# The causal mask of decayed attention: added by VectorE to the scores in place, instead of by mask products on TensorE

## The chip, the cores and the metric

The kernel runs on one core of a Trainium2 chip. The metric is the device time of one execution in microseconds (us). One launch computes a whole small network; the change touches its last stage alone, about 210 us of some 1860 us.

Engines are named as the profile names them: PE is TensorE's matrix products, PEld its weight loads (they overlap PE), DVE is VectorE, ACT is ScalarE, POOL is GpSimd, SP is the queue that issues DMAs.

## The reference, cut to what matters

The last stage computes two layers, an attention with a decay and a ternary projection, each followed by a residual sum and a layer norm. B is 8 sequences of N = 256 tokens (the layer takes them as the network has them), 128 channels, 16 heads of 8 channels:

```python
q = pi * _rotate(q, cos, sin) + (1.0 - pi) * q
k = pi * _rotate(k, cos, sin) + (1.0 - pi) * k
decay = -e * d_mat[None, :, :] / xi[:, None, None]
causal = jnp.where(pos[:, None] >= pos[None, :], 0.0, -jnp.inf)
bias = decay + causal[None, :, :]
scores = jnp.einsum('bhqd,bhkd->bhqk', q, k) * dh ** (-0.5) + bias[None]
attn = jax.nn.softmax(scores, axis=-1)
out = jnp.einsum('bhqk,bhkd->bhqd', attn, v)
return out @ w_o
# ... and then, after x = layernorm(x + out):
w_eff = ternary_quantize(weight) * alpha
out = jnp.einsum('bsd,od->bso', input, w_eff) + bias
```

The change is about `causal`, which is 0 where a key is not later than the query and minus infinity where it is.

## The kernel before, in words

The program is written by hand for each engine, as one list of instructions per engine. The engines meet through semaphores; within an engine everything runs in the order in which it is written. That order is what the change alters.

The last stage is `decayed_attention_and_ternary`. It runs eight turns, one for each sequence i. A turn does the attention of sequence i, and beside it the preparation of sequence i + 1 ("ahead") and the output and norm of sequence i - 1 ("behind"). The last turn, i = 7, has nothing ahead; there PE and DVE do the ternary layer (`weights`, `ternary`, `tern_sum`) in those places instead.

PSUM has eight banks of 512 columns. Four of them, S[0] to S[3], hold scores of sequence i for the exponentials; two, M[0] and M[1], hold scores of sequence i + 1 for the search of each row's maximum; two, X[0] and X[1], hold projections, transposes and outputs.

The 16 heads are worked in four chunks c of four heads y; the PE array's rows are split in four strips of 32, a strip for each head. For one chunk, into the four S banks:

- `shifted` (L2992) does three kinds of products. L2997 writes minus each query's maximum into 384 columns, and first waits, head by head, until ACT has read the chunk before out of that bank. L2999 adds key block 0 by all 256 queries. L3001 adds key block 1 by its 128 queries.
- `mask` (L3003) adds the mask: L3006 multiplies an identity by the 0 or -1e30 table, into two blocks of 128 columns, the two diagonal blocks. The table, `cmask16`, is bf16.
- `exp` (L3186) on ACT then takes head after head: L3189 is the exponential of the 384 columns into `prob`. It waits for `shifted`, which the mask product signals.
- `mix` (L3009) multiplies `prob` by the values; `mix(i, p, 0)` needs chunks 0 and 1, `mix(i, p, 1)` chunks 2 and 3.

For sequence i + 1, `mask_top` (L2962) and `score_top` (L2972) fill M[0] and M[1] in turn for u = 0 to 11, and DVE's `highest` (L3269; the reduction is L3276) takes the maximum. Two banks serve twelve fills, so fill u waits for reduction u - 2. `split_top` and PE's `turn_top` (L2986) turn the maxima round, and ACT's `top_row_act` (L3182) copies them negated: with that the next turn's `shifted` can start. Their inputs come from ACT's copies of the turned q and k (`copy_qk`, L3176), which stand behind `exp(i, 1)` on ACT, and from POOL's casts of these to bf16 (L2897).

For sequence i - 1, `by_token` (L3019, its transposes are L3023), DVE's `normalise` (L3286), `turn_output`, ACT's `copy_output`, `output` and the norm run between these. DVE also rotates q and k of sequence i + 2 (`rotate`, L3252, the last instructions of its turn).

In the last turn `weights` (L3297 to L3310) makes the ternary weights on DVE, `turn_weights` (L3044, L3046) transposes them on PE right behind chunk 0, and `ternary(k)` and `tern_sum(k)` do the layer for sequences 0 to 5.

Of the kernel before, what the change touches and what calls it, by code (L numbers as in the profile page):

```python
# [19 lines left out]
ALU = mybir.AluOpType  # L20
# [3 lines left out]
P = 128  # L24
B, L, D = 8, 256, 128
# [484 lines left out]
HPG = 4  # L510
# [2313 lines left out]
def decayed_attention_and_ternary(nc, net, io, out):  # L2824

    with ExitStack() as ctx:
# [4 lines left out]
        SPAN = L + P  # L2831
# [14 lines left out]
        s = open_stage(nc, net.pool, "clear:2 rate0:1 rate:1 decay:1 proj:2 v_ready:2 products:2 wide:2 turned:4 qkT:4 "  # L2846
                       "cast:4 scored:12 maxed:12 top16:1 top_parts:1 top_ps:1 top_row:1 shifted:16 exped:16 mixed:2 o_wide:2 o_ps:2 "
                       "row_inv:2 o_ready:2 oT_ps:1 oT_ready:1 " + NORM +
# [12 lines left out]
        diagonal = net.cmask16[:, 0:P]  # L2861
# [11 lines left out]
        with nc.Block() as block:  # L2873
# [63 lines left out]
            def _(pe):  # L2937
# [54 lines left out]
                def shifted(i, p, c):  # L2992
                    if c == 0:
                        pe.wait_ge(s.top_row.sem, s.top_row.at(i, 1))
                    for y in range(HPG):
                        pe.wait_ge(s.exped.sem, s.exped.at(i, HPG * (c - 1) + y + 1 if c else 0))
                        pe.matmul(S[y][:, 0:SPAN], pick[row(y), c:c + 1].to_broadcast([W, P]), top_row[row(y), :], start=True, stop=False)  # L2997
                    for y in range(HPG):
                        pe.matmul(S[y][:, 0:L], kT[p][row(y), c, 0:P], qT[p][row(y), c, :], start=False, stop=False)  # L2999
                    for y in range(HPG):  # L3000
                        pe.matmul(S[y][:, L:SPAN], kT[p][row(y), c, P:L], qT[p][row(y), c, P:L], start=False, stop=False)  # L3001

                def mask(i, c):  # L3003
                    for y in range(HPG):
                        masked = S[y].rearrange("p (h q) -> p h q", h=2)[:, :, 0:P]
                        pe.matmul(masked, net.ident16[:, :], diagonal.unsqueeze(1).to_broadcast([P, 2, P]), start=False, stop=True)\  # L3006
                            .then_inc(s.shifted.sem, 1)

# [51 lines left out]
                def run(i, p, ahead, behind):  # L3060
# [3 lines left out]
                    shifted(i, p, 0)  # L3064
                    mask(i, 0)
                    if not ahead:
# [10 lines left out]
                    shifted(i, p, 1)  # L3077
                    mask(i, 1)
                    if behind:
# [12 lines left out]
                    else:  # L3092
                        ternary(2)
                    mask(i, 2)
                    if not ahead:
# [14 lines left out]
                    if ahead:  # L3110
                        score_top(i + 1, 6, 7)
                    mask(i, 3)
                    if ahead:
# [47 lines left out]
            def _(act):  # L3161
# [24 lines left out]
                def exp(i, c, first=0, end=HPG):  # L3186
                    for y in range(first, end):
                        act.wait_ge(s.shifted.sem, s.shifted.at(i, HPG * c + y + 1))
                        act.activation(prob[:, c, y, :], S[y][:, 0:SPAN], ACT.Exp, scale=RDH ** -0.5)\  # L3189
                            .then_inc(s.exped.sem, 1)  # L3190
# [46 lines left out]
            def _(dve):  # L3237
# [88 lines left out]
                def tern_apply(k):  # L3326
# [4 lines left out]
                    last.then_inc(s.t_last.sem, 1)  # L3331

                def run(i, p, ahead, behind):
                    if not ahead:
                        weights()
                    if behind:
                        normalise(i - 1)
                    if not ahead:
                        for k in range(B - 2):
                            tern_sum(k)  # L3340
                    if ahead:
                        for u in range(8):
                            highest(i + 1, u)
                    if behind:
# [214 lines left out]
```

## Time and profile before

| | |
|---|---|
| median of 3 runs | 1860.57 us (1859.46 to 1862.26) |
| the profiled execution | 1857.45 us |
| its span, first to last instruction | 1855.6 us |
| PE, DVE, ACT, POOL busy in the span | 83%, 55%, 47%, 34% |
| mean granted clock of PE | 0.901 |

The profile is of one execution. Its span leaves out 1.85 us that lie around the instructions. The share of busy time is an average over all stages of the network, which have different limits, so what follows is read in the last stage alone, from about 1643 us to the end. "In a bracket" a timeline row says how long the engine had stood idle before it, and what ended that.

### The profile page before, as it was taken

The numbers are of one execution on the slowest core, as the hardware profiler recorded it, in microseconds if no ns is written. First come the engines' busy times: TensorE is split into PE (matmuls) and PEld (weight loads), VectorE is DVE, ScalarE is ACT, GpSimd is POOL, SyncE is SP. The second block draws the span as 40 slices with busy tenths as digits, with TensorE's granted clock in tenths as the row PEclk, the third lists the DMA queues.
The fourth block names the chain that finished last, engine by engine and source line by source line (L and its number), as shares of the span: only waits on it lengthen the run. The fifth ranks groups of instructions, "written<-read, shape, count | busy, mean of one in ns | idle before, by whom it ended". The sixth has DMA issues, their size and how long they took to land. (4 is left out here: it accounts for less than half of the span.)

```text
span 1855.6 us, 31560 instructions
## 1 busy us (share of the span) xinstructions
PE 1541.1 (83%) x11327; PEld 1143.5 (62%) x11327; DVE 1013.0 (55%) x2393; ACT 870.8 (47%) x1935; POOL 632.7 (34%) x707
## 2 busy tenths in 40 slices
PE   4699977899786999986669999999975795668996
PEld 3366664566562666665647878787763674535664
DVE  6566546565475799972246563566442121344555
ACT  5555544555457777743434445444441231225553
POOL 3487413975132587743210001000126005111113
PEclk7799988899897899996879999999986898769998
DMA  7300000000004445716160000000001102100000
GB/s 223 99 13 12 18 1 8 12 13 12 7 1 43 82 76 79 77 29 150 42 186 2 0 1 1 1 1 0 1 1 43 32 19 45 12 4 2 2 2 24
DMA packets 75278, 63.71 MB, mean 34 GB/s; under 512 B 25367, under 2 KB 62791, under 8 KB 75143
## 3 DMA queue, kind: packets, MB, share of 16 engines
q1 hardware_dynamic: 65142, 53.53, 13.8%
q0 software_dynamic: 3072, 6.30, 1.7%
q10 hardware_dynamic: 6928, 2.12, 0.5%
q8 instruction: 81, 1.33, 0.3%
q14 instruction: 55, 0.44, 0.1%
HBM read 48.09 MB, written 9.57 MB: 31 GB/s over the span
## 5 line engine op out<-in xcount | busy, mean ns | idle before, releaser
L1351 POOL TENSOR_TENSOR inject<-delta_x,b_rows 128x512 f32<-128x512 f32 x128 | 159.6, 1271 | 80.8 <-DMA b_rows<-b_rows_dram 44.7
L1609 DVE TENSOR_TENSOR_SCAN state<-bank,inject 128x512 f32<-128x512 f32 x128 | 150.3, 1205 | 7.0 <-POOL inject L1351 3.9
L2040 POOL TENSOR_TENSOR ve<-mv,eps 128x1 f32<-128x1 f32 x32 | 6.1, 190 | 340.4 <-DVE mv L2188 340.4
L1519 ACT ACTIVATE bank<-delta,a_neg 128x255 f32<-128x255 f32 x256 | 109.4, 472 | 17.2 <-DVE state L1609 16.2
L3276 DVE TENSOR_REDUCE top<-bank 128x2 f32<-128x512 f32 (+1 forms) x96 | 61.8, 685 | 71.8 <-PE bank L2978 51.0
L2149 ACT ACTIVATE Z<-bank 128x512 f32<-128x512 f32 x64 | 34.7, 595 | 129.5 <-PE bank L2102 129.5
L2725 DVE TENSOR_TENSOR shared_hid<-shared_gate,bank 128x256 f32<-128x256 f32 x64 | 26.4, 420 | 123.8 <-ACT shared_gate L2635 72.8
L2126 ACT ACTIVATE U<-bank 128x512 f32<-128x512 f32 x128 | 74.7, 593 | 40.2 <-PE bank L2063 39.1
L2576 PE MATMUL bank<-xT,sg 128*128 128x256 f32 x128 | 45.3, 437 | 52.3 <-DVE shared_hid L2725 45.8
L594 POOL TENSOR_TENSOR rotated<-rot_cos,rot_sin 128x512 f32<-128x512 f32 x56 | 70.8, 1268 | 51.2 <-DVE rot_sin L900 51.2
L600 POOL TENSOR_TENSOR inv_norm<-sum_sq,neghalf 128x16 f32<-128x16 f32 x28 | 82.0, 2929 | 4.2 <-POOL sum_sq L598 0.2
L1428 PEld LDWEIGHTS bank<-tabs,by_token 128*128 128x128 f32 x512 | 67.9, 196 | 24.9 <-issue 14.4
L637 PE MATMUL bank<-wqkv,hT 128*128 128x512 f32 x128 | 68.3, 662 | 15.2 <-ACT hT L798 11.4
L1530 ACT ACTIVATE by_token<-bank,c_cols 128x256 f32<-128x256 f32 x128 | 53.5, 468 | 44.8 <-PE bank L1408 44.7
L1432 PE MATMUL bank<-x_work,tabs 128*128 128x512 f32 x128 | 73.6, 658 | 0.0
L3189 ACT ACTIVATE prob<-bank 128x384 f32<-128x384 f32 x128 | 53.2, 501 | 36.8 <-PE bank L3006 36.8
L1428 PE MATMUL bank<-tabs,by_token 128*128 128x128 f32 x512 | 69.3, 280 | 0.0
L897 DVE TENSOR_TENSOR rot_cos<-bank,rope 128x512 f32<-128x512 f32 x64 | 43.8, 685 | 39.9 <-ACT squares L803 29.1
L2576 PEld LDWEIGHTS bank<-xT,sg 128*128 128x128 f32 x128 | 24.8, 216 | 63.9 <-DVE shared_hid L2725 52.0
L803 ACT ACTIVATE squares<-bank 128x512 f32<-128x512 f32 x64 | 38.0, 598 | 44.4 <-PE bank L637 23.3
L605 POOL TENSOR_TENSOR rotated<-rotated,inv_norm 128x512 f32<-128x512 f32 x56 | 57.2, 1042 | 2.2
L825 ACT ACTIVATE prob<-bank 128x512 f32<-128x512 f32 x64 | 34.7, 595 | 46.4 <-PE bank L684 46.4
(561 smaller groups left out, 4211.3 us busy)
## 6 DMA issues: line engine op xcount, KB each, us to landing
b_rows<-b_rows_dram SPq DMA_DIRECT2D x32, 512.0 KB, 9.2
v<-v SPq DMA_DIRECT2D x32, 130.0 KB, 2.3
slots<-zero SPq DMA_DIRECT2D x10, 256.0 KB, 3.6
rows<-slots SPq DMA_DIRECT2D x10, 256.0 KB, 4.6
moe_w<-in_L_ffn_rg_dram SPq DMA_DIRECT2D x1, 2048.0 KB, 8.7
moe_w<-in_L_ffn_ru_dram SPq DMA_DIRECT2D x1, 2048.0 KB, 14.3
wqkv<-in_L_ffn_wqkv_dram SPq DMA_DIRECT2D x2, 768.0 KB
slots_out<-y SPq DMA_DIRECT2D x8, 160.0 KB, 2.1
```

Source lines behind the costliest of these rows:

```text
L594: pool.tensor_tensor(rot[:, p, m, :], rc[:, m % 2, :], rs[:, m % 2, :], ALU.add).then_inc(s.added.sem, 1)
L600: pool.tensor_tensor(flat(rn), flat(ss), net.neghalf[:, 0:2 * LH], ALU.pow).then_inc(s.inv_norm.sem, 2)
L605: pool.tensor_tensor(r, r, rn[:, m, :].unsqueeze(2).to_broadcast([P, LH, LDH]), ALU.mult).then_inc(s.roped.sem, 1)
L637: pe.matmul(to, hT[:, p, tok(t)], w[:, j * INNER:(j + 1) * INNER], start=True, stop=True).then_inc(s.qk_ps.sem, 1)
L1351: pool.tensor_tensor(dB[:, n % R, :, :], dx[:, :, seq(n)], both(b_all[:, q % 4, n % CH, :]), ALU.mult).then_inc(s.inject.sem, 1)
L1428: last = pe.matmul(sum_bank(i)[:, c * L + t * P:c * L + (t + 1) * P], hcT[:, j % RT, t, c * P:(c + 1) * P], ident, start=(k == 0 and t == ...
L1432: last = pe.matmul(sum_bank(i)[:, :], ident, flat(hc[:, j % R, :, :]), start=False, stop=(k == NS - 1))
L1519: last = act.activation(dA[n % RD][:, c, 1:L], delta[:, c, i * L + 1:(i + 1) * L], ACT.Exp, scale=a_neg[:, c, k:k + 1])
L1609: dve.tensor_tensor_scan(flat(h[:, n % R, :, :]), flat(dA[n % RD]), flat(dB[:, n % R, :, :]), 0.0, ALU.mult, ALU.add).then_inc(s.state.sem, 1)
L2126: act.activation(U[:, m % 2, 4 * (g - 1):4 * g, :], bank[n % 2][:, :].rearrange("p (h t) -> p h t", h=4), ACT.Copy)\
L2576: pe.matmul(to[:, 0:L], w[:, c * P:(c + 1) * P], net.xT[:, i * L:(i + 1) * L], start=True, stop=True).then_inc(done.sem, 1)
L3276: dve.tensor_reduce(to, M[u % 2].rearrange("p (c k) -> p c k", c=count), AX.X, ALU.max).then_inc(s.maxed.sem, 1)
```

## The change

The mask products leave PE: `mask` and its four calls are gone there, and the last product of `shifted` now signals each head. DVE gets a `mask` of its own, which waits for each head's signal, adds the table to the same two blocks of the S bank in place, and signals `masked`, a new semaphore. ACT's exponential waits for that. In DVE's turn the four calls stand at its start, behind `normalise`, ahead of reduction 2, and ahead of reduction 6; in the last turn ahead of `weights`, behind `normalise`, and ahead of `tern_sum(2)` and `tern_sum(4)`.

```diff
--- before.py
+++ after.py
@@ -2844,7 +2844,7 @@
         o, oT = sb("o", [P, TPB, D]), sb("oT", [P, L])
         FEW = 3
         s = open_stage(nc, net.pool, "clear:2 rate0:1 rate:1 decay:1 proj:2 v_ready:2 products:2 wide:2 turned:4 qkT:4 "
-                       "cast:4 scored:12 maxed:12 top16:1 top_parts:1 top_ps:1 top_row:1 shifted:16 exped:16 mixed:2 o_wide:2 o_ps:2 "
+                       "cast:4 scored:12 maxed:12 top16:1 top_parts:1 top_ps:1 top_row:1 shifted:16 masked:16 exped:16 mixed:2 o_wide:2 o_ps:2 "
                        "row_inv:2 o_ready:2 oT_ps:1 oT_ready:1 " + NORM +
                        f" mag:1 mean_ps:1 limits:3 tern:1 wT_ps:1 wT:1 t_ps:{B} t_sum:{B} t_stats:{B} t_agg:{B} t_var:{B} t_rstd:{B} t_out:{FEW} t_last:{B - FEW}")
         above, below, mag, wT = (sb(k, [P, P]) for k in ("above", "below", "magnitude", "ternaryT"))
@@ -2998,13 +2998,7 @@
                     for y in range(HPG):
                         pe.matmul(S[y][:, 0:L], kT[p][row(y), c, 0:P], qT[p][row(y), c, :], start=False, stop=False)
                     for y in range(HPG):
-                        pe.matmul(S[y][:, L:SPAN], kT[p][row(y), c, P:L], qT[p][row(y), c, P:L], start=False, stop=False)
-
-                def mask(i, c):
-                    for y in range(HPG):
-                        masked = S[y].rearrange("p (h q) -> p h q", h=2)[:, :, 0:P]
-                        pe.matmul(masked, net.ident16[:, :], diagonal.unsqueeze(1).to_broadcast([P, 2, P]), start=False, stop=True)\
-                            .then_inc(s.shifted.sem, 1)
+                        pe.matmul(S[y][:, L:SPAN], kT[p][row(y), c, P:L], qT[p][row(y), c, P:L], start=False, stop=True).then_inc(s.shifted.sem, 1)
 
                 def mix(i, p, half):
                     pe.wait_ge(s.exped.sem, s.exped.at(i, 2 * HPG * (half + 1)))
@@ -3062,7 +3056,6 @@
                         mean()
                     turn_top(i)
                     shifted(i, p, 0)
-                    mask(i, 0)
                     if not ahead:
                         turn_weights()
                     if ahead:
@@ -3075,7 +3068,6 @@
                     if ahead:
                         mask_top(i + 1, 1)
                     shifted(i, p, 1)
-                    mask(i, 1)
                     if behind:
                         turn_output(i - 1)
                     if not ahead:
@@ -3091,7 +3083,6 @@
                         score_top(i + 1, 0, 1)
                     else:
                         ternary(2)
-                    mask(i, 2)
                     if not ahead:
                         ternary(3)
                     if ahead:
@@ -3109,7 +3100,6 @@
                     shifted(i, p, 3)
                     if ahead:
                         score_top(i + 1, 6, 7)
-                    mask(i, 3)
                     if ahead:
                         mask_top(i + 1, 6, 7)
                         pe.wait_ge(s.qkT.sem, s.qkT.at(i + 1, 4))
@@ -3185,7 +3175,7 @@
 
                 def exp(i, c, first=0, end=HPG):
                     for y in range(first, end):
-                        act.wait_ge(s.shifted.sem, s.shifted.at(i, HPG * c + y + 1))
+                        act.wait_ge(s.masked.sem, s.masked.at(i, HPG * c + y + 1))
                         act.activation(prob[:, c, y, :], S[y][:, 0:SPAN], ACT.Exp, scale=RDH ** -0.5)\
                             .then_inc(s.exped.sem, 1)
 
@@ -3330,16 +3320,28 @@
                         last = dve.tensor_scalar(of, of, t_mv[:, t, 0:1], t_rstd[:, t:t + 1], ALU.subtract, ALU.mult)
                     last.then_inc(s.t_last.sem, 1)
 
+                def mask(i, c):
+                    for y in range(HPG):
+                        dve.wait_ge(s.shifted.sem, s.shifted.at(i, HPG * c + y + 1))
+                        of = S[y].rearrange("p (h q) -> p h q", h=2)[:, :, 0:P]
+                        dve.tensor_tensor(of, of, diagonal.unsqueeze(1).to_broadcast([P, 2, P]), ALU.add).then_inc(s.masked.sem, 1)
+
                 def run(i, p, ahead, behind):
+                    mask(i, 0)
                     if not ahead:
                         weights()
                     if behind:
                         normalise(i - 1)
+                    mask(i, 1)
                     if not ahead:
                         for k in range(B - 2):
+                            if k in (2, 4):
+                                mask(i, 1 + k // 2)
                             tern_sum(k)
                     if ahead:
                         for u in range(8):
+                            if u in (2, 6):
+                                mask(i, 2 + u // 4)
                             highest(i + 1, u)
                     if behind:
                         norm_stats(dve, s, n, i - 1, y_tok)
```

The order of DVE's instructions in a middle turn before, from behind `rotate` to the norm's first part (`bank` is a PSUM bank):

```order
L3290 RECIPROCAL inv<-bank 128x16 x2
L3294 TENSOR_TENSOR o<-bank,inv 128x128 x2
L3276 TENSOR_REDUCE top<-bank 128x4 x4
L3276 TENSOR_REDUCE top<-bank 128x2 x4
L160 BN_STATS n_st<-bank 128x6 x2
L166 BN_AGGR n_mv<-n_st 128x2 x2
L3276 TENSOR_REDUCE top<-bank 128x2 x2
L177 TENSOR_SCALAR n_xn<-bank,n_mv,n_rstd 128x128 x2
L3276 TENSOR_REDUCE top<-bank 128x2 x2
```

and the same stretch of the changed kernel, where L3280 is the old L3290, L3284 the old L3294, L3266 the old L3276, and L3327 is the mask:

```order
L3327 TENSOR_TENSOR bank<-bank,cmask 128x2x128 x4
L3280 RECIPROCAL inv<-bank 128x16 x2
L3284 TENSOR_TENSOR o<-bank,inv 128x128 x2
L3327 TENSOR_TENSOR bank<-bank,cmask 128x2x128 x4
L3266 TENSOR_REDUCE top<-bank 128x4 x2
L3327 TENSOR_TENSOR bank<-bank,cmask 128x2x128 x4
L3266 TENSOR_REDUCE top<-bank 128x4 x2
L3266 TENSOR_REDUCE top<-bank 128x2 x2
L3327 TENSOR_TENSOR bank<-bank,cmask 128x2x128 x4
L3266 TENSOR_REDUCE top<-bank 128x2 x2
L160 BN_STATS n_st<-bank 128x6 x2
L166 BN_AGGR n_mv<-n_st 128x2 x2
```

Sixteen mask additions came in at four places: the first four stand directly behind `rotate`, two groups among the reductions.

The start of DVE's last turn before (L3300 to L3310 are `weights`):

```order
L3300 TENSOR_SCALAR delta<-bank 128x1
L3301 TENSOR_SCALAR minus_delta<-bank 128x1
L3303 TENSOR_SCALAR above<-w_in,delta 128x128
L3304 TENSOR_SCALAR below<-w_in,minus_delta 128x128
L3306 TENSOR_TENSOR above<-above,below 128x128
L3308 TENSOR_SCALAR above<-above,w_in 128x128
L3310 TENSOR_TENSOR ternaryT<-bank,tabs 128x128
L3290 RECIPROCAL inv<-bank 128x16 x2
L3294 TENSOR_TENSOR o<-bank,inv 128x128 x2
L3315 TENSOR_TENSOR x_tok<-bank,w_in 128x256
L3319 BN_STATS t_st<-x_tok 128x6 x2
L3323 BN_AGGR t_mv<-t_st 128x2 x2
```

and changed (L3290 to L3300 are `weights`):

```order
L3327 TENSOR_TENSOR bank<-bank,cmask 128x2x128 x4
L3290 TENSOR_SCALAR delta<-bank 128x1
L3291 TENSOR_SCALAR minus_delta<-bank 128x1
L3293 TENSOR_SCALAR above<-w_in,delta 128x128
L3294 TENSOR_SCALAR below<-w_in,minus_delta 128x128
L3296 TENSOR_TENSOR above<-above,below 128x128
L3298 TENSOR_SCALAR above<-above,w_in 128x128
L3300 TENSOR_TENSOR ternaryT<-bank,tabs 128x128
L3280 RECIPROCAL inv<-bank 128x16 x2
L3284 TENSOR_TENSOR o<-bank,inv 128x128 x2
L3327 TENSOR_TENSOR bank<-bank,cmask 128x2x128 x4
L3305 TENSOR_TENSOR x_tok<-bank,w_in 128x256
```

The first chunk's additions moved in ahead of the ternary weights, the second chunk's ahead of the first sums.

## Rows read from the trace of the kernel before

**Rows 1.** The page of the whole run: busy time by engine.

```profile
PE 1541.1 (83%) x11327; PEld 1143.5 (62%) x11327; DVE 1013.0 (55%) x2393; ACT 870.8 (47%) x1935; POOL 632.7 (34%) x707
```

**Rows 2.** Stretches: us, length, busy PE, PEld, DVE, ACT, POOL, granted clock, DMA.

```profile
1753.13:1775.58 22.45, 20.51 (x247) 13.57 (x247) 12.16 (x38) 11.88 (x31) 3.23 (x6) 1.00 0.01 1
1820.48:1855.60 35.12, 21.66 (x233) 16.75 (x233) 17.24 (x74) 9.77 (x23) 13.81 (x26) 0.81 0.11 31
```

**Rows 3.** Chain of waits, last stage: shares by line, one piece (start, us).

```profile
by line: DVE top L3276 14.5%; PE bank L3006 7.9%; PE bank L3014 6.9%; PE bank L2984 6.9%; PE bank L2968 6.8%; ACT prob L3189 5.2%; PE bank L2953 4.6%; issue 4.3%; PE bank L2999 3.7%; PE bank L3023 3.2%; PE bank L2997 3.2%; PE bank L3016 3.0
...
1777.12 0.54 PE bank L3006 x4
```

**Rows 4.** Timeline, a middle turn: start, us, engine, line [idle before <-releaser].

```profile
1754.29 0.39 PE L3001 MATMUL bank<-moe_w 32*128 32x128 f32 x8
...
1754.61 0.61 PE L3006 MATMUL bank<-cmask,ident 128*128 128x256 bf16 x4
...
1754.85 0.22 DVE L3267 TENSOR_TENSOR qk_wide<-prod 128x64 f32<-128x64 f32 x1
1754.93 1.64 ACT L3189 ACTIVATE prob<-bank 128x384 f32<-128x384 f32 x4 [0.90 <-PE bank L3006]
...
1755.27 1.04 PE L3023 MATMUL bank<-tabs,out_wide 128*128 128x128 f32 x8
...
1756.45 0.26 PEld L2997 LDWEIGHTS bank<-minus_top,pick 32*128 32x128 bf16 x4 [0.32 <-ACT prob L3189]
...
1757.16 0.45 PE L3001 MATMUL bank<-moe_w 32*128 32x128 f32 x8
...
1757.86 0.49 ACT L3189 ACTIVATE prob<-bank 128x384 f32<-128x384 f32 x1 [1.29 <-PE bank L3006]
...
1761.80 0.23 PEld L2978 LDWEIGHTS bank<-k,q 32*128 32x128 bf16 x8 [1.02 <-POOL q L2897]
```

**Rows 5.** Timeline of that turn, second half, VectorE's reductions.

```profile
1762.23 1.29 DVE L3276 TENSOR_REDUCE top<-bank 128x4 f32<-128x512 f32 x2 [5.29 <-PE bank L2978]
...
1764.42 1.29 DVE L3276 TENSOR_REDUCE top<-bank 128x4 f32<-128x512 f32 x2 [0.90 <-PE bank L2978]
...
1766.48 1.29 DVE L3276 TENSOR_REDUCE top<-bank 128x2 f32<-128x512 f32 x2 [0.77 <-PE bank L2968]
...
1768.98 1.29 DVE L3276 TENSOR_REDUCE top<-bank 128x2 f32<-128x512 f32 x2 [1.21 <-PE bank L2968]
```

**Rows 6.** VectorE's groups by line and form: total busy, mean ns of one.

```profile
L3276 DVE TENSOR_REDUCE top<-bank 128x2 f32<-128x512 f32 x64 | 41.2, 685 | 20.8 <-PE bank L2968 20.8
...
L1176 DVE SCALAR_TENSOR_TENSOR u<-bank,b1a,gate 128x256 f32<-128x256 f32 x32 | 15.4, 483 | 13.3 <-ACT gate L1068 12.6
...
L3294 DVE TENSOR_TENSOR o<-bank,inv 128x128 f32<-128x128 f32 x16 | 3.4, 252 | 0.0
L3315 DVE TENSOR_TENSOR x_tok<-bank,w_in 128x256 f32<-128x256 f32 x8 | 3.3, 415 | 5.5 <-PE bank L3057 5.5
```

**Rows 7.** Timeline of the last turn.

```profile
1819.92 0.16 DVE L3300 TENSOR_SCALAR delta<-bank 128x1 f32<-128x1 f32 x1
...
1821.03 0.29 DVE L3308 TENSOR_SCALAR above<-above,w_in 128x128 f32<-128x128 f32 x1
...
1821.63 0.49 PE L3001 MATMUL bank<-moe_w 32*128 32x128 f32 x8
...
1822.67 0.23 PEld L3046 LDWEIGHTS bank<-tabs,above 128*128 128x128 f32 x1
...
1823.09 1.92 PE L3023 MATMUL bank<-tabs,out_wide 128*128 128x128 f32 x8
...
1836.12 0.46 DVE L160 BATCH_NORM_STATS2 n_st<-bank 128x6 f32<-128x128 f32 x2
```

**Rows 8.** Busy time and granted clock, two single microseconds of the last turn.

```profile
1819.00:1820.00 1.00, 0.46 (x3) 1.00 0.03 8
...
1822.00:1823.00 1.00, 1.00 (x9) 0.50 0.00 0
```

## The prediction

> **What bounds the kernel now.** I read the page first: PE is busy 83% of the span and DVE 55% [rows 1], which invites moving work from PE to DVE. Only the last stage changes, so I went to its stretches: a middle turn takes 22.45 us, with PE busy 20.51 and DVE 12.16 at full clock [rows 2]. The reader is to see there that PE has only 1.94 us free, and DVE 10.3. By shares alone the change looks right. Third, the chain of waits: the mask products L3006 hold 7.9% of the stage, in pieces of four that take 0.54 us, but the reductions L3276 hold 14.5% and the exponentials 5.2% [rows 3]. So the chain hops between PE, ACT and DVE, and what counts is when each hands over. That I read last, in the timeline of one turn, and the sum is made on it.
>
> In its first half the turn is paced by handovers PE to ACT to PE. Chunk 0's exponentials start 0.32 us after the first mask product (1754.61 to 1754.93), run one every 0.383 us ((1.64 - 0.49) / 3), and end at 1756.57; chunk 1's first products stood idle 0.32 us for them. Chunk 1's exponentials (from 1757.86) gate ACT's copies, these gate POOL's casts, and PE idles 1.02 us for the cast at 1761.80 [rows 4]. In its second half PE and DVE play ping-pong over two M banks: DVE reduces a pair (1.29 us), idles 0.90, 0.77 and 1.21 us while PE fills again, and so on [rows 5].
>
> **Price of one mask.** No row shows a DVE addition in place in PSUM of 2x128 elements. The nearest is L3315, PSUM plus table, 256 elements, 415 ns. A half as long one takes 252 ns (L3294), another op of 256 elements 483 ns (L1176) [rows 6]. I take 0.42 us, the row of its own kind and size, and keep 0.25 and 0.48 as ends. Two reductions of 0.685 us take 1.29 together [rows 5, 6], so one starts 0.08 before the last ends, though each has a semaphore wait; I give the masks the same: one every 0.34 us, four in 1.43. That is shorter than the exponentials' 0.383, so behind the first mask ACT keeps its pace.
>
> The Trainium skill, "VectorE: DVE Perf Modes", section Terms, speaks against that: every DVE op is followed by a flush, and the next can't issue before the pipe is empty. By it four masks would take 1.68 us; the trace shows an overlap of 0.08 at each pair, so I follow the trace. By the page's rule the sum below would be some 6 us larger.
>
> **The change part by part, middle turn.** For a handover with DVE idle I take 0.05 us from PE to DVE, 0.42, and 0.06 from DVE to ACT; PE to ACT was about 0.05 as well (the first mask product needs 0.27 of the 0.32). Head 0's last product is done about when its mask product began (1754.6), so a free handover costs 0.53 where it cost 0.32: +0.21.
>
> 1. Chunk 0. DVE isn't free: the masks stand behind `rotate`, whose last instruction ends at 1755.07 [rows 4]. Masks start 1754.99, exponentials 1755.47 instead of 1754.93: +0.54. PE's products of chunk 1 need head 3's exponential, which moves from 1756.57 to 1757.11. PE saves the 0.43 us in which it issued four mask products, but only waits longer. L3001 of chunk 1 then ends at 1758.15 instead of 1757.61 [rows 4].
> 2. Chunk 1. `normalise` fits in between (DVE has it done by 1757.2). Masks start about 1758.12, exponentials 1758.60 instead of 1757.86 [rows 4]: +0.74 in all. Copies, casts and the products behind them go with it: L2978 at 1762.54, reduction 0 at 1762.97.
> 3. Chunk 2. Its scores lie ready from about 1761.7, but its masks are queued behind reductions 0 and 1 on DVE. They run 1764.18 to 1765.61. Exponentials start at 1764.65, not late for `mix`. But reduction 2, whose scores are there at about 1765.2, waits for DVE until 1765.53: it was 1764.42 [rows 5], +1.11. The gap of 0.90 was there to be filled, and four masks are 1.43 less the overlap, so 0.44 spills over. Then PE's `mix` and the scores behind it take part of it up: reduction 4 goes from 1766.48 to 1767.37, +0.89.
> 4. Chunk 3. Reduction 5 ends at 1768.66, masks run 1768.58 to 1770.01, exponentials start 0.5 late, which `mix` of chunk 3 absorbs. The gap there was 1.21 [rows 5], so reduction 6 starts at 1769.93 instead of 1768.98: +0.95. From there all is as before: reductions 8 to 11, norm, `split_top`, `turn_top`.
>
> A middle turn: +0.94, 23.39 us. The 1.7 us that PE saves (4 x 0.43) are all spent in waits: where PE was the one waited for (behind chunk 2's masks, `turn` comes 0.34 sooner against the rest), DVE is now later. Seven turns have something ahead; the first lacks `normalise` but has `rotate`, exponentials and reductions in the same places: 7 x 0.94 = +6.6.
>
> **Last turn.** `weights` started on DVE at 1819.92 and ended at 1821.32, well before PE wanted it (L3046 at 1822.67) [rows 7]. Now it is queued behind chunk 0's four masks, which can't start before L3001 ends at 1822.12 [rows 7]. Four masks to 1823.5, `weights` 1.40 more: L3046 at 1824.94, +2.27. Queued behind it on PE are `by_token` and chunk 1; all wait. Chunk 1's exponentials add a free handover, about 2.4 late. Then DVE is the bound: the sums 0 to 5 (1.14 us each) share it with 12 masks (4.1 us) of which only part falls into its gaps. Followed through: sums 0 and 1 from 1829.7, masks of chunk 2 1832.0, sums 2 and 3 1833.3, masks of chunk 3 1835.95 (these now wait for PE), sums 4 and 5 1837.3, norm of sequence 6 at 1839.6 instead of 1836.12 [rows 7]: +3.45. What follows to the end (norm, POOL's applications, last sequence) hangs on that norm, unchanged.
>
> PE's clock: in this turn PE was busy only 0.46 in a microsecond at 1819 and the clock was at its lower level (1.2 GHz, 0.50) at 1822 [rows 8]; eight L3023 took 1.92 there against 1.04 at full clock [rows 4, 7]. The new stall of 2.8 us at 1822.1 should keep it low for longer: 0 to 0.9 us more, I take 0.35. The Trainium skill, "TensorE: Matmul & The Clock Gate", section "The HAM clock gate", has it that throttling follows idleness and activity lifts it; rows 8 agree, and if it bit in every middle turn too, that is a rival below. Last turn: +3.8.
>
> **Sum.** 6.6 + 3.8 = +10.4 on the profiled execution's 1857.45: 1867.9. That execution lies 3.1 below the median of the runs shown, so against the median I forecast 1860.57 + 10.4 = 1871.0, 0.56% slower. (0.2% is 3.7 us, about what a measurement of this kernel can tell from no change.)
>
> **Range.** With masks at 0.25 us: chunk 0 +0.37, chunk 1 +0.04 more, four masks then take 0.76 and fit the gaps, in all +0.45 a turn, and the last turn +2.5: +5.7, 1866.3. With 0.48 and no overlap: a mask every 0.48 is slower than the exponentials, chunk 0 +0.9, chunk 1 +0.27, the two later groups 0.5 each beyond step 3 and 4: +2.1 a turn, +5.5 at the end: +20, 1881. I give 1865 to 1881.
>
> **Rivals.**
> - Faster: PE is the bound, as its 20.51 of 22.45 us say, and the 7.9% of L3006 in the chain come back. Mechanism: at each of the four places in a turn the engine behind it takes up PE's 0.43 us. 8 x 4 x 0.43 = -13.8: 1846.8. For it: rows 2 and 3. Against it: behind each of these pieces stands an exponential or a reduction that now needs DVE first. It decides at the price of a mask: a handover through DVE beats the old one only below about 0.21 us, and all rows of 256 elements are at twice that. 5%.
> - No change: masks of 0.25 us or less whose gaps hold them all, while ACT and PE close up behind `rotate`: 0 to +3.7, say 1862. For it: DVE has 10.3 us free in a turn. Against it: chunk 0 starts late even then. 8%.
> - A dearer mask (a PSUM write in place that costs more, or no overlap behind the waits): up to 1881, as above. 14%.
> - The clock falls in each middle turn, since PE's free time grows from 1.94 to about 4.6 us (20.51 - 1.7 = 18.8 of 23.39). A stretch like the 3 us at the last turn costs up to 1.5 us (half of it), 7 times: +10.4 more, 1881. Against it: a busy share near 0.8 in bits shorter than those of 1818 to 1821. 8%.
> - That the change doesn't do what it says I rule out: the order of DVE shows the 16 additions a turn, and the diff takes L3006 out of PE.
> My forecast has the other 65%.
>
> Faster 0.06, same 0.08, slower 0.86: the first rival and a little over, the second, the rest.
>
> **What would show it.** Turns of 23.4 us; DVE busy about 17.5 us a turn (12.16 + 4 x 1.34); a mask near 0.42 us, starts 0.34 apart; first exponentials of chunk 0 about 0.9 us behind L3001's end; DVE without a gap from reduction 0 to reduction 3; in the last turn PE idle some 2.8 us before the weights' transpose, released by DVE. Wrong if turns stay at 22.45 or shrink, if masks take under 0.3 or over 0.5 us, or if the granted clock in middle turns leaves 1.00.

## The result, and the profile after

The changed kernel takes 1871.61 us (median of 5 runs, 1870.96 to 1873.47) against 1860.60 (1859.46 to 1863.07): +11.0 us, ratio 1.0056, 95% interval 1.0042 to 1.0070. It is slower, by more than a measurement of it is uncertain. The forecast was 1871.0.

The page first; PE and DVE as in [rows 1]:

```profile
PE 1540.4 (82%) x11198; PEld 1135.7 (61%) x11199; DVE 1054.4 (56%) x2521; ACT 870.7 (47%) x1935; POOL 632.8 (34%) x707
```

PE has hardly lost anything in sum, DVE has gained 41 us. Then three stretches, with the columns of [rows 2]: the first turn, a middle turn, and the last turn with the end.

```profile
1663.71:1688.55 24.84, 20.36 (x213) 10.98 (x211) 14.94 (x42) 11.19 (x29) 2.32 (x4) 0.89 0.00 1
1758.56:1781.90 23.34, 20.21 (x231) 12.35 (x231) 17.27 (x54) 11.85 (x31) 3.23 (x6) 1.00 0.01 2
1828.58:1869.80 41.22, 23.41 (x220) 18.28 (x220) 23.02 (x93) 9.66 (x23) 13.85 (x26) 0.72 0.09 26
```

A middle turn went from 22.45 to 23.34 us. PE is busy 20.21 us of it (20.51 before), DVE 17.27 (12.16 before). The first turn has 24.84 us (22.50 before), and its mean granted clock is 0.89 (0.95 before). All turns here and below are read between the starts that the chain of waits gives to `turn_top`'s products; in the first turn that is 0.2 us behind the first product, in every kernel. The last turn to the end has 41.22 us; before it was 35.70.

The chain of waits of the sixth turn, with the 2 us ahead of it (1780 to 1804):

```profile
by line: DVE top L3266 24.1%; ACT prob L3179 13.7%; DVE bank L3327 8.8%; PE bank L3008 8.3%; PE bank L2968 5.8%; PE bank L2984 5.8%; issue 5.6%; PE bank L3010 3.6%; PE bank L2978 3.1%; POOL q L2897 2.6%; PE bank L2989 2.3%; ACT moe_w L3170 
...
1784.80 1.65 ACT prob L3179 x4
...
1797.99 1.33 DVE bank L3327 x4
```

[rows 3] has the whole stage; the same turn of the kernel before has:

```profile
by line: DVE top L3276 17.2%; PE bank L3006 9.6%; PE bank L3014 8.9%; PE bank L2968 7.8%; PE bank L2984 6.5%; ACT prob L3189 5.1%; issue 4.0%; PE bank L2989 4.0%; PE bank L3016 3.9%; PE bank L2953 3.9%; PE bank L3023 3.9%; PE bank L2999 3.8
```

The mask line stands in the chain much as L3006 did (8.8%; 9.6% then), but the exponentials behind it went from 5.1% to 13.7% and the reductions from 17.2% to 24.1%. (Taken over exactly one turn in both, the exponentials go from 5.1% to 14.1% and the reductions from 17.4% to 21.8%.) The chain now runs more over ACT and DVE.

The timeline of the fifth turn, which starts at 1758.56 (that of [rows 4] at 1752.55):

```profile
1760.29 0.39 PE L3001 MATMUL bank<-moe_w 32*128 32x128 f32 x8
...
1761.00 1.42 DVE L3327 TENSOR_TENSOR bank<-bank,cmask 128x256 f32<-128x256 f32 x4
1761.46 1.64 ACT L3179 ACTIVATE prob<-bank 128x384 f32<-128x384 f32 x4 [1.42 <-DVE bank L3327]
...
1763.15 0.09 PEld L2997 LDWEIGHTS bank<-minus_top,pick 32*128 32x128 bf16 x1 [0.29 <-ACT prob L3179]
...
1764.10 1.43 DVE L3327 TENSOR_TENSOR bank<-bank,cmask 128x256 f32<-128x256 f32 x4 [0.94 <-PE bank L3001]
...
1764.57 0.49 ACT L3179 ACTIVATE prob<-bank 128x384 f32<-128x384 f32 x1 [1.48 <-DVE bank L3327]
...
1768.35 0.23 PEld L2978 LDWEIGHTS bank<-k,q 32*128 32x128 bf16 x8 [1.01 <-POOL q L2897]
```

Counted from the turn's start, chunk 0's exponentials begin at 2.90 us (2.38 before), chunk 1's at 6.01 (5.31). PE now stands idle before each of chunk 1's heads, for ACT. The load for the first scores of the maxima stands at 9.79 (9.25).

Its second half, DVE alone, for [rows 5]:

```profile
1768.78 1.29 DVE L3266 TENSOR_REDUCE top<-bank 128x4 f32<-128x512 f32 x2 [3.25 <-PE bank L2978]
...
1769.99 1.42 DVE L3327 TENSOR_TENSOR bank<-bank,cmask 128x256 f32<-128x256 f32 x4
...
1771.32 1.27 DVE L3266 TENSOR_REDUCE top<-bank 128x4 f32<-128x512 f32 x2
...
1773.36 1.29 DVE L3266 TENSOR_REDUCE top<-bank 128x2 f32<-128x512 f32 x2 [0.77 <-PE bank L2968]
...
1774.57 1.42 DVE L3327 TENSOR_TENSOR bank<-bank,cmask 128x256 f32<-128x256 f32 x4
...
1775.89 1.28 DVE L3266 TENSOR_REDUCE top<-bank 128x2 f32<-128x512 f32 x2
```

The reductions 0, 2, 4 and 6 stand at 10.22, 12.76, 14.80 and 17.33 us (9.68, 11.87, 13.93, 16.43 before): +0.54, +0.89, +0.87, +0.90. No bracket stands before reductions 2 and 6: DVE had no idle time before them, where it had 0.90 and 1.21 us.

The last turn, for [rows 7], which starts at 1828.58 (before at 1819.90):

```profile
1830.86 0.64 PE L3001 MATMUL bank<-moe_w 32*128 32x128 f32 x8
1831.53 1.43 DVE L3327 TENSOR_TENSOR bank<-bank,cmask 128x256 f32<-128x256 f32 x4 [3.00 <-PE bank L3001]
...
1833.95 0.29 DVE L3298 TENSOR_SCALAR above<-above,w_in 128x128 f32<-128x128 f32 x1
1834.29 0.18 PEld L3040 LDWEIGHTS bank<-tabs,above 128*128 128x128 f32 x1 [3.09 <-DVE above L3298]
...
1834.56 1.91 PE L3017 MATMUL bank<-tabs,out_wide 128*128 128x128 f32 x8
...
1849.34 0.46 DVE L160 BATCH_NORM_STATS2 n_st<-bank 128x6 f32<-128x128 f32 x2
```

PE's weight load stood idle 3.09 us for DVE's weights before the transpose L3040 (the old L3046), its products 2.79 us. And the clock, with the columns of [rows 8]; 1829 and 1832 first, then two stretches of 2 us in the first turn:

```profile
1829.00:1830.00 1.00, 0.42 (x6) 0.80 0.00 0
...
1832.00:1833.00 1.00, 0.00 (x0) 0.50 0.00 0
```

```profile
1681.00:1683.00 2.00, 0.98 (x6) 0.96 0.00 0
1683.00:1685.00 2.00, 2.00 (x25) 0.50 0.00 0
```

In the last turn the lower clock begins at 1829.6, before chunk 0's scores, and lasts to 1839.8; before the change it was from 1821.8 to 1825.2. In the first turn PE was busy 0.98 of 2 us and then ran at the lower level for some 3.4 us. Before the change the clock did not fall in this turn, although PE was hardly busier at the same place of it (1.01 of the 2 us from 1679, granted clock 1.00). What differs is one wait: 1.22 us at 1681.79 after the change, 0.76 at 1680.01 before.

### The profile page after: what moved, and what is told of

Its sections match the earlier page's. It is cut to its first block and busy times, and to the rows that moved or that the text cites. A ratio compares the mean times of both kernels' runs of the same rounds, so it can differ in the third digit from the quotient of the medians.

```text
span 1869.8 us, 31432 instructions
## 1 busy us (share of the span) xinstructions
PE 1540.4 (82%) x11198; PEld 1135.7 (61%) x11199; DVE 1054.4 (56%) x2521; ACT 870.7 (47%) x1935; POOL 632.8 (34%) x707
## 3 DMA queue, kind: packets, MB, share of 16 engines
q1 hardware_dynamic: 65142, 53.53, 13.2%
## 5 line engine op out<-in xcount | busy, mean ns | idle before, releaser
L3266 DVE TENSOR_REDUCE top<-bank 128x2 f32<-128x512 f32 (+1 forms) x96 | 61.7, 683 | 42.2 <-PE bank L2978 28.3
L1428 PEld LDWEIGHTS bank<-tabs,by_token 128*128 128x128 f32 x512 | 67.8, 196 | 24.6 <-issue 14.1
```

The costliest lines, as they stand in the source:

```text
L1428: last = pe.matmul(sum_bank(i)[:, c * L + t * P:c * L + (t + 1) * P], hcT[:, j % RT, t, c * P:(c + 1) * P], ident, start=(k == 0 and t == ...
L3266: dve.tensor_reduce(to, M[u % 2].rearrange("p (c k) -> p c k", c=count), AX.X, ALU.max).then_inc(s.maxed.sem, 1)
```

## The experiments

All take the last stage apart. Times of the whole come from three chips: on one the kernel before takes 1860.3 us, on the two others 1782.0 and 1782.5. The difference lies ahead of the last stage. Both kernels, profiled again on the third chip, had the same middle turns to 0.01 us and the same first and last turns to 0.2 us (the first two rows below), so turns compare across chips and whole times only as ratios to the kernel before on the same chip. "Stage" is from the first `turn_top` to the end of the span, which is known to 0.05 us. Turns and stages are those of one profiled execution.

| kernel | turn 0 | a middle turn | last turn and end | stage | ratio of the whole, 95% |
|---|---|---|---|---|---|
| before | 22.50 / 22.41 | 22.45 / 22.45 | 35.70 / 35.75 | 192.9 / 192.8 | 1 |
| changed | 24.84 / 24.74 | 23.34 / 23.34 | 41.22 / 41.40 | 206.1 / 206.2 | 1.0056 (1.0042 to 1.0070) |
| no mask | 21.44 | 21.31 | 33.22 | 182.5 | 0.9946 (0.9927 to 0.9966) |
| DVE chunks 0, 1 | 24.43 | 22.99 | 39.77 | 202.4 | 1.0053 (1.0039 to 1.0068) |
| DVE chunks 2, 3 | 24.27 | 22.81 | 38.46 | 199.8 | 1.0039 (1.0023 to 1.0054) |
| weights first | 24.84 | 23.35 | 38.47 | 203.4 | 1.0050 (1.0033 to 1.0068) |
| half mask | 22.02 | 22.20 | 38.33 | 193.6 | 1.0028 (1.0012 to 1.0045) |
| chunk 2 early | 24.35 | 22.96 | 41.88 | 205.6 | 1.0066 (1.0044 to 1.0087) |
| PE, moved | 21.87 | 22.08 | 35.68 | 190.0 | 0.9984 (0.9968 to 1.0000) |
| PE, alternating | 22.42 | 22.97 | 35.69 | 196.0 | 1.0027 (1.0013 to 1.0042) |
| PE, chunk 0 first | 21.99 | 21.85 | 35.65 | 188.8 | 0.9981 (0.9971 to 0.9990) |
| PE, grouped first | 22.04 | 21.75 | 34.19 | 186.7 | 0.9974 (0.9962 to 0.9985) |

The first two rows give the first pair of profiles and the second. Where the first turn begins differs between the profiled executions by 5 us on the first chip (1662.7 to 1668.1) and by 7 on the two others (1583.0 to 1590.4), which is why ratios are blunter than stages. One middle turn of "DVE chunks 0, 1" and one of "DVE chunks 2, 3" is 0.2 us longer than the others (23.21 and 23.02), for a reason that stays open.

**Both kernels again, on the third chip, unaltered.**

> The kernel before, unaltered, for its turns on this chip and in this execution: 22.45 us a turn, whatever the time of the whole is. If the turn differs here, the turns of the runs before must be set against it.

> The changed kernel, unaltered, as a second look at its turns, its first turn and its last: 23.34 us a middle turn; if the lower clock in the first turn (24.84 there against 22.50 before) comes from the change and not from chance, it is there again; the last turn 5 to 6 us longer than before.

Met: 22.45 and 23.34. The first turn had 24.74, with the granted clock at 0.50 for 3.4 us from 19 us into it, as in the first pair, and the last turn +5.65. So the clock's fall in the first turn comes with the change and not by chance.

**No mask at all.** What was removed, without what was added.

```diff
-                        act.wait_ge(s.masked.sem, s.masked.at(i, HPG * c + y + 1))
+                        act.wait_ge(s.shifted.sem, s.shifted.at(i, HPG * c + y + 1))
 def mask(i, c):   # DVE
-    ...
+    pass
```

> The causal mask is left out altogether: PE's mask products are gone and DVE adds nothing, the exponentials wait for the scores alone. It parts the change into what was taken away and what was added. My theory (PE, ACT and DVE hand over to each other, PE's 0.43 us count only where PE is the one waited for): chunks 0 and 1 hand over 0.27 us sooner each, chunk 3's products leave the gap between reductions 5 and 6 (0.43), so a middle turn of about 21.5 us against 22.45, in all -8 us, 1852.6. Rival, PE is the bound: each of the 4 x 0.43 us comes back, a turn of 20.7 us, -14, 1847. Second rival, the products were hidden: 0 to -2. In the first case the addition on DVE cost about 19 us of which the removal gave 8 back.

A turn of 21.31 us: 1.14 less than before, between the two theories (0.95 and 1.75) and much nearer the first. In DVE's timeline the gap ahead of reduction 6 is now 0.77 where it was 1.21 [rows 5]:

```profile
1744.86 1.29 DVE L3266 TENSOR_REDUCE top<-bank 128x2 f32<-128x512 f32 x2 [0.77 <-PE bank L2968]
1746.92 1.29 DVE L3266 TENSOR_REDUCE top<-bank 128x2 f32<-128x512 f32 x2 [0.77 <-PE bank L2968]
```

So of the 1.72 us of PE's mask products in a turn (4 x 0.43) 1.14 were on the path: about 0.6 in the two handovers of the first half (reduction 0 at 9.06 us of the turn instead of 9.68), 0.44 ahead of reduction 6, 0.1 ahead of reduction 2. In the stage the removal gives 10.4 us and the addition takes 23.6.

**Half of the chunks on DVE.** The edit, shown for chunks 0 and 1; PE masks the others as before, and ACT waits for `masked` or `shifted` by chunk. The second run has (2, 3).

```diff
                         last = pe.matmul(S[y][:, L:SPAN], ...)
+                        if c in (0, 1):
+                            last.then_inc(s.shifted.sem, 1)
 def mask(i, c):   # PE, as before the change
+    if c in (0, 1):
+        return
 def mask(i, c):   # DVE, as in the changed kernel
+    if c not in (0, 1):
+        return
```

> Chunks 0 and 1 masked by DVE as in the changed kernel, chunks 2 and 3 by PE as before. Theory (the cost sits in the late handover behind rotate and in the first half of a turn, and in the weights' stall of the last turn): a middle turn of 22.99 us (+0.54, what reduction 0 was late in the changed kernel's trace), the weights' transpose late as in the changed kernel, +7 in all, 1867.5. Rival (DVE's added time counts, wherever it stands): half of the change's +11, 1866, with the middle turn at 22.9 and the last turn's stall no larger than half.

> Chunks 2 and 3 masked by DVE, 0 and 1 by PE as before. Theory (most of these masks fall into the gaps in which DVE waits for PE's refill): reduction 0 not late, reduction 2 some 0.35 us, a middle turn of 22.75 us (+0.3), no stall of the weights, the sums of the last turn about 1 us late: +3, 1863.6; with the run before it this adds up to the +11. Rival (DVE's added time counts wherever it stands): +5.5, 1866.

The turns are 22.99 (as expected to 0.01) and 22.81 (0.06 above), and their excesses, 0.54 and 0.36, add up to the changed kernel's 0.89. The rival, that DVE's added time counts wherever it stands, gives 0.45 for each and falls, since turns repeat to 0.01 us. But my whole times were too low, by 2.7 and 5.1 us (1870.18 and 1868.66 measured): both kernels have the first turn of 24.3 to 24.4 us (the clock again), and chunks 2 and 3 alone cost 2.8 us in the last turn, where I had expected 1.

**The weights ahead of chunk 0's masks** in the last turn, on DVE.

```diff
-    mask(i, 0)
     if not ahead:
         weights()            # all but the last addition
+    mask(i, 0)
+    if not ahead:
+        weights_turned()     # the last addition
```

> The changed kernel with the ternary weights made on DVE ahead of chunk 0's masks of the last turn, and only their transposed copy behind them. Theory (the +5.5 us of the last turn are largely PE's stall of 2.9 us behind the weights and the lower clock after it): the weights' transpose starts some 2.3 us sooner, the clock is back at its upper level sooner, -3 against the changed kernel, 1868.6. Rival (in the last turn DVE's sum of work is the bound, the order doesn't matter): 0, 1871.6.

The last turn went from 41.22 to 38.47 us, -2.75, as the theory said; the turns before it are the same. It still is 2.8 us longer than before the change. In the whole time (ratio 1.0050 against 1.0056) the gain can't be told.

**Half a mask.**

```diff
-dve.tensor_tensor(of, of, diagonal.unsqueeze(1).to_broadcast([P, 2, P]), ALU.add)
+dve.tensor_tensor(of[:, 0:1, :], of[:, 0:1, :], diagonal.unsqueeze(1), ALU.add)
```

> The changed kernel with DVE's additions halved: only the first of the two diagonal blocks (128 of 256 elements) is masked, key block 1's mask is left out. Waits, order and number of instructions stay. Theory (an addition counts by its length: 0.15 us at each of the two handovers of the first half, and the groups of four shrink from 1.43 to about 0.9 us, which fits into the gaps between reductions): mask 0.28 us, 0.2 apart, a middle turn of 22.8 us (+0.38 to +0.45 where the whole mask gave +0.89), about 1867. Rival (the semaphore round through a third engine is the cost, not the arithmetic): the turn stays near 23.3, 1871.

The turn is 22.20 us: 1.14 below the changed kernel and even 0.25 below the kernel before. The rival is out. The theory had the sign wrong against the kernel before. One addition takes 0.290 us, a group of four 0.88:

```profile
L3327 DVE TENSOR_TENSOR bank<-bank,cmask x128: 275/290/300, 1585.7 to 1754.7; 128x128 f32<-128x128 f32 x128
```

```profile
1641.47 1.29 DVE L3266 TENSOR_REDUCE top<-bank 128x2 f32<-128x512 f32 x2 [0.77 <-PE bank L2968]
1642.67 0.88 DVE L3327 TENSOR_TENSOR bank<-bank,cmask 128x128 f32<-128x128 f32 x4
1643.53 1.29 DVE L3266 TENSOR_REDUCE top<-bank 128x2 f32<-128x512 f32 x2
```

Reduction 6 stands right behind the masks, 2.06 us behind reduction 4; before it was 2.50 [rows 5]. The four masks just fit into the gap although PE, rid of its own, had shortened that gap to 0.77. I had counted DVE's additions as hidden there, but not that the removal of PE's products then comes through. Between this addition (0.290 us, -0.25) and the whole one (0.423 us, +0.89) a straight line crosses zero at 0.32 us; no run lies between them, so this is an estimate, and one of a middle turn alone. The whole is still slower than before the change (ratio 1.0028), as the last turn stays 2.6 us longer.

**Chunk 2's masks ahead of reduction 0** on DVE.

```diff
-if u in (2, 6):
-    mask(i, 2 + u // 4)
+if u in (0, 6):
+    mask(i, 2 + u // 6)
```

> The changed kernel with chunk 2's masks ahead of reduction 0 on DVE instead of behind reduction 1. Their scores lie ready about 1 us before reduction 0's. Theory as far as the changed kernel's trace goes (reduction 4 is gated by PE's mix and scores as much as by reduction 3): reductions 0 and 1 up to 0.15 us late, 2 and 3 some 0.2 us sooner, a middle turn between 23.1 and 23.35. Rival (my step 3, 0.44 us spill over at this place): the turn loses 0.35 us, 23.0, 1869.

The turn is 22.96: the rival was right, my reading of PE as a second gate was wrong. The masks now fill an idle stretch of DVE, and reduction 0 is late by 0.05 us only:

```profile
1646.49 1.43 DVE L3327 TENSOR_TENSOR bank<-bank,cmask 128x256 f32<-128x256 f32 x4 [1.97 <-PE bank L3001]
1647.82 1.28 DVE L3266 TENSOR_REDUCE top<-bank 128x4 f32<-128x512 f32 x2
1649.91 1.29 DVE L3266 TENSOR_REDUCE top<-bank 128x4 f32<-128x512 f32 x2 [0.81 <-PE bank L2978]
```

With reduction 2 at 12.36 us of the turn instead of 12.76, reduction 4 came 0.38 sooner too. So of the +0.89, 0.38 was this one place in DVE's order. The whole time is too blunt to show it (1.0066, 1.0044 to 1.0087). The profiled execution is the slowest of its six, and one of its middle turns has 24.53 us: the granted clock is 0.50 there from 1725.2 to 1728.6, after PE had been busy 1.45 of 2 us. So the clock can fall in a middle turn too; the changed kernel has a stretch just as busy (1.45 of 2 us at 1752) with the clock at 1.00.

**Masks on PE, moved.** Back to the kernel before, with two calls moved in PE's list.

```diff
+mask(i, 2)
 if ahead:
     score_top(i + 1, 0, 1)
-mask(i, 2)
 ...
     score_top(i + 1, 6, 7)
-mask(i, 3)
-if ahead:
     mask_top(i + 1, 6, 7)
+mask(i, 3)
```

> The kernel before, masks on PE, only their place in PE's list altered: chunk 2's ahead of the scores for reductions 0 and 1 (PE idles 1.02 us there for the cast), chunk 3's behind the mask products for reductions 6 and 7. Theory (chunk 3's four products stand in the gap that reduction 6 waits for; chunk 2's cost almost nothing where they were): reduction 6 sooner by up to 0.43 us, a middle turn of 22.0 to 22.1 us, -3, 1857.5. Rival (PE is the bound and works the same): 22.45, 1860.3.

22.08 us a turn, as expected: 0.37 less, with the same work on every engine. The rival falls.

**Masks as the first products.** The mask, now over all 384 columns, starts the accumulation for chunks 0, 1 and 2. Chunk 0's four masks stand together, ahead of the wait for the maxima; those of chunks 1 and 2 alternate with the maxima's products, head by head (shown). Chunk 3's stand as in "moved".

```diff
 for y in range(HPG):
     pe.wait_ge(s.exped.sem, ...)
+    pe.matmul(S[y][:, 0:SPAN], net.ident16[:, :], net.cmask16[:, 0:SPAN], start=True, stop=False)
-    pe.matmul(S[y][:, 0:SPAN], pick..., top_row..., start=True, stop=False)
+    pe.matmul(S[y][:, 0:SPAN], pick..., top_row..., start=False, stop=False)
```

> Masks on PE, where it idles: for chunks 0, 1 and 2 the mask is the first product of the group (identity by the 384-column table, start of the accumulation), for chunk 0 while PE waits for the negated maxima, for chunks 1 and 2 head by head while it waits for the exponentials; the last score product signals. Chunk 3's mask products stand behind the mask products for reductions 6 and 7. Theory: the handovers to ACT come 0.27 us sooner at chunks 0 and 1 (0.11 to 0.16 of it given back at chunk 1, as one more product stands behind the last exponential), 0.43 us sooner at chunk 3: a middle turn of 21.5 to 21.7 us, near the 21.31 of no mask at all, -6 to -7, 1853.5. Rival (what no mask gained was PE's work, not its place): a turn near 22.4.

Wrong by 1.4 us: 22.97 a turn, slower than before. PE's weight loads in chunk 1 show where it goes (L2994 loads all 128 rows for the mask, L3010 a 32-row strip for the maxima):

```profile
1662.21 0.10 PEld L2994 LDWEIGHTS bank<-cmask,ident 128*128 128x128 bf16 x1 [0.17 <-ACT prob L3203]
...
1662.48 0.09 PEld L3010 LDWEIGHTS bank<-minus_top,pick 32*128 32x128 bf16 x1 [0.17 <-issue]
...
1662.75 0.10 PEld L2994 LDWEIGHTS bank<-cmask,ident 128*128 128x128 bf16 x1 [0.17 <-issue]
...
1663.01 0.09 PEld L3010 LDWEIGHTS bank<-minus_top,pick 32*128 32x128 bf16 x1 [0.17 <-issue]
```

Each load is 0.27 us behind the last, and PE's weight load is idle 0.17 before it, three times of four for nothing that the profile shows ("issue"). Four L3006 in a row, of 256 columns, had come 0.11 apart; masks of 384 columns in a row come 0.16 apart (chunk 0 of the last kernel below), and the loads of four strips nearly together.

**The same, grouped.** Two kernels: only chunk 0's masks first (chunks 1 to 3 as in "moved"), and chunks 0, 1 and 2 first, but the four masks of a chunk ahead of its four other products.

```diff
 for y in range(HPG):
     pe.wait_ge(s.exped.sem, ...)
     pe.matmul(S[y][:, 0:SPAN], net.ident16[:, :], net.cmask16[:, 0:SPAN], start=True, stop=False)
+for y in range(HPG):
     pe.matmul(S[y][:, 0:SPAN], pick..., top_row..., start=False, stop=False)
```

> Masks on PE: chunk 0's as the first four products (384-column table, start of the accumulation) while PE waits for the negated maxima; chunks 1 and 2 behind the scores as before (chunk 2's ahead of the scores of reductions 0 and 1), chunk 3's behind the mask products for reductions 6 and 7. No product of all 128 rows stands between products of 32-row strips that did not before. Theory (each switch between the two kinds of weight load leaves PE idle for about 0.17 us, which spoilt the run with masks head by head; chunk 0's handover gains 0.23, chunk 3's place 0.37): a middle turn of 21.85 us, -5 us of the whole, ratio 0.997. Rival (chunk 0's gain is lost again in the wait for chunk 1): 22.08 as with the masks only moved, ratio 0.998.

> As the run with masks first for chunks 0, 1 and 2 (a middle turn of 22.97 us), with the same products and the same four waits, but the four masks of a chunk stand together ahead of the four products of the maxima instead of alternating with them. Two switches between full and strip weight loads a chunk instead of eight. Theory (the switch is the cost, about 0.27 us from a full product to the next strip load): chunk 1 and chunk 2 come about 0.9 us sooner each, of which chunk 1's counts in full, a middle turn of 22.0 to 22.1 us. Rival (the wider mask and its place behind the exponentials are the cost): 22.8 or more.

21.85 for the first, as expected. 21.75 for the second, 1.22 less than with the same products alternating and lower than the 22.0 that I gave it. The 0.27 us from a mask's load to a strip's is paid once a chunk:

```profile
1656.09 0.53 PEld L2996 LDWEIGHTS bank<-cmask,ident 128*128 128x128 bf16 x4
1656.94 0.10 PEld L3011 LDWEIGHTS bank<-minus_top,pick 32*128 32x128 bf16 x4 [0.32 <-ACT minus_top L3199]
...
1659.66 0.10 PEld L2996 LDWEIGHTS bank<-cmask,ident 128*128 128x128 bf16 x1 [0.20 <-ACT prob L3204]
1659.93 0.10 PEld L3011 LDWEIGHTS bank<-minus_top,pick 32*128 32x128 bf16 x4 [0.18 <-issue]
```

Chunk 0's masks run while PE waits for the maxima, chunk 1's while it waits for the exponentials, the last of them behind the last exponential. So the place of the masks relative to the strips is what counts. The 1.22 us have two parts that no run separates: the idle 0.17 at each switch, and that the four strip products, which here run side by side (four within 0.34 us at 1659.93), have a stretch each when masks stand between them.

With its end 1.5 us shorter too this kernel has the shortest stage of all that mask in full, 186.7 us. Of the whole it takes 0.9974 of the kernel before (0.9962 to 0.9985), which is clear of the changed one but overlaps "moved" and "chunk 0 first". DVE has no part in it.

## Why the prediction was right, point by point

**Right: the mechanism of the middle turn**, handovers in its first half and DVE's groups among the reductions in its second. The price of a mask was 0.423 us (0.42 taken), four took 1.43 with the overlap of 0.08. Against the flush rule of the Trainium skill ("VectorE: DVE Perf Modes", section Terms), which would give 1.68 by that estimate, the trace was the better guide: masks start 0.34 apart though each waits on a semaphore. The free handover and the place behind `rotate` gave +0.52 at chunk 0 (+0.54 forecast). Reduction 6 was 0.90 late (0.95 forecast), and a turn grew 0.89 (0.94 forecast). That the halves add, 0.54 and 0.36, was shown by masking two chunks at a time. The first rival, PE as the bound, is out: without any mask the turn fell by 1.14, not 1.72, and with DVE's masks it rose.

**Right in kind, off in size: two terms that cancelled.** For the first half I had +0.74 at reduction 0, it was +0.54. Chunk 1's exponentials are 0.70 late, but before, ACT had waited between the first and the second of them for the transposed output; that wait took 0.17 of it up. In the second half I let PE's `mix` and scores take back 0.22 between reductions 2 and 4 (from +1.11 to +0.89). They took back 0.02: 2.05 us lie between the two, 2.06 before. What chunk 2's masks added ahead of reduction 2 was 0.35 (0.37 forecast). So the turn's +0.94 came out near 0.89 partly by luck, 0.20 too much in the first half against 0.20 too little in the second.

**The term that was mis-sized: the last turn**, +3.8 forecast, +5.5 measured (+5.65 in the second pair). The stall behind the weights was there and, undone by the order of two calls, gave 2.75 back. But the norm of sequence 6 came 4.5 us late against 3.45 + 0.35: the clock fell 1.0 us after the turn's start instead of 1.9, before chunk 0's scores, and stayed low for 10.2 us instead of 3.4. Another 1.0 us lies behind that norm, where the clock was low from 1853.5 to 1856.9 (it was high at that place before) and eight L3017 took 1.77 us against 1.09.

**The term that was missing: the first turn**, +2.34 where I counted +0.94. The clock fell there to its lower level, which costs about 1.4 of the 2.34 us. I had put the clock's fall in all middle turns at 8%. It came in the first turn, where PE has no output of a sequence behind to work on, in all six profiles of kernels with whole masks on DVE and in none of the eight with masks on PE alone, without mask, or with half masks. What sets it off stays open. The Trainium skill ("TensorE: Matmul & The Clock Gate", section "The HAM clock gate") has idleness before the fall. The traces don't settle it: PE was busy 0.98 of the 2 us before, and 1.01 of 2 us in the kernel before, where the clock stayed up. I had also counted PE busy for 18.8 us of a changed turn; it was 20.21, so its free time grew from 1.94 to 3.1 us and not to 4.6, which spoke less for this rival than I thought.

**Where the number was lucky.** The stage grew by 13.2 us in the profiled executions (2.34 in the first turn, 6 x 0.89, 5.5 in the last; 13.4 in the second pair) against my 10.4, 2.8 too little. The medians of the whole differ by 11.0. The 2.2 us between must lie ahead of the stage, where nothing was changed: the stage began 1.0 us later with the change in the first pair of profiles and 1.1 us sooner in the second, and its start scatters by 5 us and more. So 1871.0 against 1871.61 is closer than the working deserves. The stage's growth is shown; the whole's is known as 4.2 to 7.0 permille.

**Wrong: the low end of the price.** For a mask of 0.25 us I had +0.45 a turn and break-even below 0.21. At 0.29 the turn was 0.25 us shorter. What failed there is the sentence that the 1.7 us PE saves "are all spent in waits": ahead of reduction 6 0.44 us of it come back as soon as DVE's masks fit into the gap, and 0.09 ahead of reduction 2. And chunk 2's place in DVE's list was worth 0.38 us a turn, which step 3 had as a spill of 0.44 and which my expectation for that run wrongly took back.

## What to carry to other kernels

Busy shares tell which engine has room, not whether a hop over it is free: a step that a second engine waits for costs the hop and whatever stands ahead of it in the helper's list. Before moving work to an emptier engine, move it to an idle stretch of its own: the same masks on PE, put where PE was waiting anyway, gave 0.7 us a turn. Price the removal and the addition apart, and look at turns, not only at whole times.

## What the runs showed of the hardware that I had not expected

Alternating products with 128-row weights and products on 32-row strips cost 0.27 us from one load to the next, 0.17 of it idle for no wait that the profile shows, where the same masks in a row came 0.16 us apart and the loads of four strips together. Eight such switches in each of two chunks made a turn 1.22 us longer than two (22.97 against 21.75).

The same program took 1860 us on one chip and 1782 on another, with the middle turns of this stage equal to 0.01 us; what differs lies ahead of the stage and was not followed up.
